# A Hyena block with a gated MLP on one core: VectorE computes the column scales of W_in ahead of the second batch's statistics

## What is computed

```python
xn = layernorm(x)                       # first normalisation
# attention part: a second layernorm, an input projection, two gated causal convolutions
h = layernorm(xn) * gamma + beta
proj = h @ W_in + b_in                  # 256 -> 768: v, x1, x2
y = v
for k, xi in ((k0, x1), (k1, x2)):
    y = causal_conv(y, k) * xi          # along time, one filter per channel
attn = xn + y @ W_out + b_out
# feed-forward part, weights are integers scaled by 1/127
ffn = (silu(xn @ wg.T) * (xn @ wu.T)) @ wd.T
return x + attn + ffn
```

## Time and profile before

| | |
|---|---|
| three timed runs | 331.23, 332.60, 333.25 us; median 332.6 us |
| profiled execution, device time | 331.48 us |
| its span in the profile | 329.6 us |
| PE busy | 302.8 us (92%) |
| DVE busy | 261.1 us (79%) |
| POOL busy | 210.4 us (64%) |
| ACT busy | 178.8 us (54%) |
| mean granted TensorE clock | 0.98 |

### The profile page before, as it was taken

One profiled execution on the slowest core, in us unless ns is written; L12 is line 12 of the kernel. 1 busy time (PEld: TensorE's weight loads), 2 busy tenths in 40 slices (PEclk: granted clock), 3 DMA queues, 4 the chain that ended last, 5 costly groups with the idle time before them and its releaser, 6 DMA issues.

```text
span 329.6 us, 11864 instructions
## 1 busy us (share of the span) xinstructions
PE 302.8 (92%) x4945; PEld 238.2 (72%) x4945; DVE 261.1 (79%) x486; ACT 178.8 (54%) x385; POOL 210.4 (64%) x290
## 2 busy tenths in 40 slices
PE   0479999999999999999999999999999999989993
PEld 0268788887777877777787777777777866668982
DVE  2789999986975887695796889779687777879994
ACT  2776599546454344443534535454445453579991
POOL 4699979278886887788777767767877663100000
PEclk9959999999999999999999999999999999999998
DMA  7994016738986968778696877869688798002344
GB/s 229 351 349 91 3 43 228 308 121 326 361 315 246 379 226 340 256 298 329 231 386 219 338 293 272 346 231 388 223 316 322 259 378 307 6 0 67 128 159 165
DMA packets 22033, 81.01 MB, mean 246 GB/s; under 512 B 1494, under 2 KB 13402, under 8 KB 13786
## 3 DMA queue, kind: packets, MB, share of 16 engines
q1 hardware_dynamic: 19458, 77.47, 63.0%
q0 software_dynamic: 2368, 2.36, 3.7%
q10 hardware_dynamic: 152, 0.40, 0.4%
HBM read 75.50 MB, written 4.72 MB: 243 GB/s over the span
## 4 chain that ended last, share of the span: by engine, by line
PE 53%; DVE 17%; POOL 10%; ACT 8%; issue 6%; DMA 3%; SPq 0%; POOLq 0%; DVEq 0%
PE bank_c L320 15%; PE bank_p L320 11%; PE bank_g L320 9%; PE bank_u L320 9%; PE bank_d L320 8%; ACT vx L834 3%; ACT vx L826 3%; DVE sgh L1041 3%; DMA res<-in_L_attn_x 3%; DVE hhl L1046 2%; DVE vx L902 2%; POOL ybuf L1360 2%; POOL vhl L1274 2%; ACT hhl L756 1%; POOL res L1308 1%
## 5 line engine op out<-in xcount | busy, mean ns | idle before, releaser
L320 PE MATMUL bank_d<-wd,hhl 128*128 128x256 f16 x384 | 84.3, 271 | 0.3 <-DVE hhl L1046 0.2
L320 PEld LDWEIGHTS bank_p<-wq,xT 128*128 128x128 f16 x1536 | 70.1, 98 | 18.3 <-issue 3.5
L320 PE MATMUL bank_p<-wq,xT 128*128 128x64 f16 x1536 | 79.6, 193 | 1.8 <-POOL wq L1313 1.8
L320 PE MATMUL bank_g<-xT,wgu 128*128 128x512 f16 x192 | 66.2, 377 | 0.5 <-ACT sgh L750 0.5
L320 PE MATMUL bank_u<-xT,wgu 128*128 128x512 f16 x192 | 66.2, 378 | 0.4 <-DVE sgh L1041 0.4
L320 PEld LDWEIGHTS bank_c<-ybuf,bands 128*128 128x128 f16 x1024 | 51.8, 96 | 16.6
L320 PEld LDWEIGHTS bank_c<-vhl,bands 128*128 128x128 f16 x1024 | 48.9, 96 | 19.5 <-issue 4.2
L320 PE MATMUL bank_c<-ybuf,bands 128*128 128x64 f16 (+3 forms) x1024 | 60.3, 184 | 0.0
L320 PE MATMUL bank_c<-vhl,bands 128*128 128x64 f16 (+3 forms) x1024 | 57.3, 184 | 2.8 <-POOL vhl L1274 1.2
L756 ACT CAST hhl<-sgh 128x512 f16<-128x512 f32 x48 | 29.7, 618 | 49.4 <-DVE sgh L1041 49.4
L1046 DVE TENSOR_TENSOR hhl<-sgh,hhl 128x512 f16<-128x512 f32 x48 | 43.8, 912 | 13.3 <-ACT hhl L756 12.1
(11 more groups left out here) (188 smaller groups left out, 547.2 us busy)
## 6 DMA issues: line engine op xcount, KB each, us to landing
bands<-taps_seq SPq DMA_DIRECT2D x64, 1024.0 KB, 8.2
out<-res SPq DMA_DIRECT2D x8, 512.0 KB, 2.9
res<-in_L_attn_x SPq DMA_DIRECT2D x3, 1024.0 KB, 10.9
res<-in_L_attn_x SPq DMA_DIRECT2D x2, 512.0 KB, 6.2
bands<-in_L_attn_W_in SPq DMA_DIRECT2D x1, 768.0 KB, 6.4
wgu<-in_L_ffn_w_gate POOLq DMA_DIRECT2D x1, 768.0 KB, 8.8
wgu<-in_L_ffn_w_up POOLq DMA_DIRECT2D x1, 768.0 KB, 10.0
wd<-in_L_ffn_w_down POOLq DMA_DIRECT2D x2, 384.0 KB, 10.4
```

Source lines behind the costliest of these rows:

```text
L320: return nc.tensor.matmul(o, w, m, start=start, stop=stop, skip_group_check=True)
```

## The change

The function `column_scales` is cut in two. The part up to `scl` keeps its name, and the two multiplications of W_in become `scale_input_weights`. In DVE's program the scales are now made between the statistics of the first batch (`pair_stats(0)`, `pair_stats(1)`) and those of the second (`pair_stats(2)`, `pair_stats(3)`); the multiplications keep their place behind the second batch's statistics. All instructions and waits stay as they are.

```diff
                 link(last)
                 link(nc.vector.tensor_scalar(scl.bitcast(I32), tsq.bitcast(I32), 1, EXPONENT, ALU.logical_shift_right, ALU.bitwise_and))
                 nc.vector.tensor_scalar(scl.bitcast(I32), scl.bitcast(I32), -1.0, float(205 << 23), ALU.mult, ALU.add).then_inc(scl_ready, 1)
+
+            def scale_input_weights():
                 dve.wait_ge(scl_ready, 1)
-
                 for k in range(KD):
                     nc.vector.scalar_tensor_tensor(out=wgm[:, k, :], in0=win[:, k, :], scalar=gb[:, 0, k:k + 1], in1=scl,
                                                    op0=ALU.mult, op1=ALU.mult).then_inc(wgs_ready[k], 1)
...
-            for j in range(4):
-                pair_stats(j)
+            pair_stats(0)
+            pair_stats(1)
             column_scales()
+            pair_stats(2)
+            pair_stats(3)
+            scale_input_weights()
```

## The result

The changed kernel takes 336.18 us (median of 4 runs, 335.69 to 336.46) against 332.14 us for the kernel before (median of 4), a ratio of 1.011 with a 95% interval of 1.0076 to 1.0144. The same kernel timed once more in the experiments gave 334.93 us (10 runs) against 332.21 us (27 runs of the kernel before), a ratio of 1.0083 (1.0056 to 1.0109). Both intervals lie clear of 1, so it is slower, by 4.0 us in the first set of runs and by 2.7 us in the second. The forecast was 335.6 us, +3.0.

A forecast was written before the change was run, and what follows sets the result against it. The prediction took the chain through DVE's second-batch statistics and POOL's line to PE's first projection as the bound. +3.1 us there, less 0.1 absorbed, gave +3.0: 332.6 to 335.6 us, range 333.2 to 337.6.

The forecast's parts named there:

- Scales no earlier than PE's column sums: DVE's column scales must wait for PE's column sums, starting at about 11.02, 0.29 us earlier; gain costed at nothing.
- End of the statistics: DVE's second-batch statistics, behind idle time and column scales, end at 14.48 in place of 11.40, +3.08 us.
- POOL's scales beside both L926: POOL's second-batch scales collide with DVE's two multiplications: bounds +1.85 and +3.45 us, taken as +3.1.
- The middle value, +2.6: POOL's power reads in the gap between DVE's two multiplications, so its scales end at about 17.2.
- The queue behind: POOL's integer issues, second scales and L1313 all move along; projections start at 24.8, with 24.0 to 25.2 around it.
- The others hidden: ACT's casts of the weights, at about 19.4 to 21.0, stay hidden by 2 us ahead of POOL's need.
- The clock: PE's clock: the same 4.5 us of half speed assumed behind the later start of the projections.
- Does it last: PE has little slack after 24 us: 0.1 us off for absorption, up to 0.5 us left in the range.
- (a): Whole delay and more, from +3.3 us, by the collision's high bound, late W_in or late clock; chance 0.35.
- (b): Partly absorbed, +1 to +2.4 us: POOL's scales without collision, or the clock back at 26.26 as before; chance 0.16.
- (c): No loss or a gain, -0.1 to +0.9 us: no collision and the clock back at the old moment; chance 0.04.
- (d): DVE cannot make the scales early: their input comes 0.9 us after the statistics' data; held true in every case.

The follow-up runs named there:

- the second experiment: Against the changed kernel, the two multiplications of W_in moved from in front of DVE's step 1 to behind its step 2; 334.18 us, ratio 1.0059 to the kernel before.
- the third: Against the changed kernel, the two multiplications of W_in also put in front of the second batch's statistics; 335.41 us, ratio 1.0108 to the kernel before.
- e1: Same kernel as the second experiment: the changed kernel with the multiplications of W_in behind DVE's step 2; 334.18 us, ratio 1.0059 to the kernel before.

## Why the prediction was right, step by step

The bound was read correctly: 2.9 us of the loss enter through the end of the statistics and POOL's line. The steps against the first profile of each:

- *Scales no earlier than PE's column sums.* Forecast 11.02, measured 10.90. The worth of having them early, forecast at nothing: the time did not follow the weights in either direction (multiplied 2.4 us later in the second experiment, 1.2 us sooner in the third).
- *End of the statistics.* Forecast +3.08, measured +2.92 (14.40 against 11.48 at POOL). Of the difference 0.12 us is the earlier start of the column scales. This is nearly the whole loss.
- *POOL's scales beside both L926.* Taken as +3.1 at their end, near the high bound; measured +3.01 (17.66 against 14.65). The two held instructions cost 0.69 and 0.64 us more than free, and the second experiment gave back those 1.3 us when the collision was removed. The middle value, +2.6, by which the power would get its reads in between, did not happen. But the kernel before had a collision of nearly that size, 1.2 us, of which the prediction named only L1244's 0.75; the rest was 0.33 on L1243 beside L922 and 0.14 on L1242. So the collision adds only 0.1 us to the difference of the two kernels; it is a price that both pay.
- *The queue behind.* The integer issues, the second scales and L1317 took 7.0 us from 17.60 to 24.59, as in the old order (14.60 to 21.60). My guess that the first issue might be 0.3 shorter away from L926 was wrong: it took 1.08 again, with DVE's L927 over since 16.16. First projection: forecast 24.8, measured 24.73.
- *The others hidden.* ACT's casts were over at 20.78, 2.2 us ahead of POOL's need; forecast 2.
- *The clock.* The same time at half speed was assumed behind the later start. The stretch came out 0.7 us longer in the mean of the profiles (5.78 against 5.06), a term that the sum had at nothing; whether it belongs to the change is open, as said above.
- *Does it last.* PE's wait for DVE's reversal shrank from 0.83 to 0.51 us, so 0.3 was absorbed; forecast 0.1, with up to 0.5 in the range. PE's timeline of the changed kernel, in answer to the last line of the earlier trace rows:

```profile
44.92 0.83 PE L320 MATMUL bank_c<-wq,xr 128*128 128x256 f16 x6 [0.51 <-DVE xr L895]
```

- *The sum.* Over the three and four profiles the means of the first projection are 21.86 and 24.76, +2.90; of the first convolution 67.76 and 71.10, +3.3; of the spans 330.3 and 333.5, +3.2. The +3.3 is 2.9 of start and 0.7 of half-speed stretch, less 0.3 absorbed. Forecast +3.0; timed +4.0 and +2.7 in the two sets of runs.

So the mechanism was right, and the closeness of the number is partly luck. In the profiles a term taken at nothing (+0.7) and one taken too small (0.3 absorbed for 0.1) nearly cancel. In the first set of runs the change was +4.0, 1.0 us more than forecast; the time of 336.18 lies only 0.6 from the 335.6 because the forecast stood on a median of 332.6 for the kernel before, which is 332.14 with one more run. No run tells why the two sets differ by 1.3 us; their intervals overlap.

Of the rivals, (a), the whole of it and more, began at +3.3: by size the first set of runs, +4.0, falls to it and the second, +2.7, to the forecast. The mechanisms that it named did not bring it there as far as the profiles show: the collision stayed at +3.0 and under its bound of +3.45, and W_in was not late; the clock's return may have a share. (b) had two ways. POOL's scales without a collision are out by the 0.89 and 1.69 us, and a clock that comes back at the same moment as before is out too: in none of the four profiles of the changed kernel did the full-speed groups begin by 26.3. (c) needed both. Rival (d) was true as a statement: DVE sat idle until the column sums.

What I had not seen ahead is how much two terms move a single profile: the hole by up to 1.3 us and the half-speed stretch by up to 1.5, against an effect of about 3.

## What to carry to other kernels

Moving work ahead of an instruction on an in-order engine is worth at most the time by which its own input is there earlier than its old turn (here 0.4 us, and nobody waited for it); check that before the gain, and then ask who waits for the instruction that is pushed back. A small instruction that feeds a long in-order queue on another engine (here 0.65 us statistics, with 10 us of POOL behind them) should go first even if its engine looks free for something larger. And when two profiles differ by more than the landmark of the change, profile both kernels again before giving the rest a cause.

## What the runs showed of the hardware that I had not expected

DVE instructions with two tensors in SBUF and POOL instructions that read SBUF held each other back, and the one under way won: POOL's L1245 took 0.89 in place of 0.20 us, ending with the first L927; DVE's L940 1.89 in place of 0.95 behind POOL's L1313. The Trainium skill ("SBUF — State Buffer", section "SBUF: two separate sides") has this as an exclusive lock, and these cases agree with it. POOL's power is the exception: once started it does not keep DVE out (L1253 at 18.89 beside L940, 0.95 us; the same in both further profiles of the kernel before, 0.94 us each), but it must wait for its own reads (1.69 us in place of 1.05).

Two tensors in SBUF are not needed for it. In the kernel before, POOL's third small instruction took 0.53 us in place of 0.20 beside DVE's L922 of the earlier trace rows (12.95 to 13.51), which reads one tensor; and in the kernel with the weights behind step 2 (`e1`), DVE's L857, a TENSOR_SCALAR on one tensor of 4 columns, took 0.82 in place of 0.17 and ended 0.03 us after POOL's L1318. POOL's timeline of the kernel before:

```profile
13.03 0.53 POOL L1243 TENSOR_TENSOR lns<-stats,lns 128x4 f32<-128x4 f32 x1
```

The profile's record of the granted clock is not complete. In the first profile of the kernel before it showed the fall and the return. In that of the changed kernel the window reads:

```profile
26.00:27.00 1.00, 1.00 (x7) 0.90 (x6) 0.17 (x1) 0.00 (x0) 0.83 (x3) 1.00 1.83 345
```

It says 1.00, while the six matmuls of 256 columns that run from 25.02 to 26.49 take 1.47 us as a group, as they did at 0.50 in the kernel before, against 0.82 at full speed. In the two further profiles of the kernel before and in all four of the changed one the record says 1.00 from 15 to 30 us, with the same 1.47 us. Read the clock from the length of like groups, not from this column alone.
